# Decay matrices of a gated delta rule on one core: where the per-row factor and its sign are applied

## The reference, cut to what matters

```
S  = S * exp(g_t);  delta = (v_t - k_t.S) * beta_t
S  = S + k_t (x) delta;  o_t = q_t.S          # per head, 8 heads of 128x128
q, k = l2norm(q), l2norm(k);  beta = sigmoid(b);  g = -exp(A_log) * softplus(a + dt_bias)
```

## Time and profile before

| what | value |
|---|---|
| median of 3 runs | 2754.35 us (2753.29 to 2766.41) |
| the profiled execution | 2753.51 us, its span 2751.7 us |
| PE busy | 2447.3 us, 89% of the span |
| DVE busy | 2025.2 us, 74% |
| ACT busy | 1136.2 us, 41% |
| POOL busy | 312.1 us, 11% |
| of POOL, the products of L1251 (64) | 92.3 us, 1475 ns each |
| mean granted TensorE clock | 0.92 of full speed |
| chain that ended last, by engine | PE 57%, DVE 23%, issue 13%, ACT 3%, POOL 1% |

### The profile page before, as it was taken

The page is one execution under the profiler, slowest core; times in us unless marked ns, Lnnn a source line. Parts: engine busy times, 40 slices in busy tenths (PEclk is TensorE's granted clock), DMA queues, the critical chain, the costliest instruction groups (busy, mean ns, idle before and its releaser), DMA issues.

```text
span 2751.7 us, 48745 instructions
## 1 busy us (share of the span) xinstructions
PE 2447.3 (89%) x15408; PEld 1603.4 (58%) x15408; DVE 2025.2 (74%) x6361; ACT 1136.2 (41%) x2066; POOL 312.1 (11%) x236
## 2 busy tenths in 40 slices
PE   2989989898998987898899899899899899899898
PEld 1434444443444444686586586586586586577576
DVE  4858677685867667768768767867867867976976
ACT  0142232313232234446446446446445435545544
POOL 1000000000000002022021121110210211211211
PEclk9989989897988988998998998999999999999899
DMA  5230312213131221201201201201101101211211
GB/s 157 79 94 29 107 41 81 56 62 83 35 109 42 83 55 58 66 14 53 68 9 55 70 2 62 66 6 62 55 17 62 47 25 39 63 32 32 63 39 31
DMA packets 158271, 152.01 MB, mean 55 GB/s; under 512 B 81128, under 2 KB 122672, under 8 KB 157520
## 3 DMA queue, kind: packets, MB, share of 16 engines
q1 hardware_dynamic: 155024, 142.83, 18.0%
q10 hardware_dynamic: 3008, 6.36, 0.6%
HBM read 121.29 MB, written 27.85 MB: 54 GB/s over the span
## 4 chain that ended last, share of the span: by engine, by line
PE 57%; DVE 23%; issue 13%; ACT 3%; DMA 2%; POOL 1%; SPq 1%; DVEq 0%; ACTq 0%; POOLq 0%
PE bank L910 5%; PE bank L922 5%; PE bank L592 4%; PE bank L580 4%; PE bank L583 3%; PE bank L648 3%; DVE arena L1609 3%; PE bank L608 3%; PE bank L502 3%; DVE arena L1667 2%; DVE arena L1665 2%; PE bank L897 2%; DVE arena L1621 2%; PE bank L879 2%; PE bank L870 2%
## 5 line engine op out<-in xcount | busy, mean ns | idle before, releaser
L922 PEld LDWEIGHTS bank<-wring,arena 128*128 128x128 f32 x2048 | 275.6, 199 | 134.6 <-issue 97.3
L1168 ACT ACTIVATE arena<-bank,w_b 128x512 f32<-128x512 f32 x256 | 175.3, 687 | 363.6 <-PE bank L910 363.2
L910 PE MATMUL bank<-arena,wring 128*128 128x512 f32 x512 | 294.1, 661 | 28.7 <-ACT arena L1168 28.6
L922 PE MATMUL bank<-wring,arena 128*128 128x128 f32 x2048 | 281.1, 284 | 22.2 <-DVE arena L1782 15.2
L1609 DVE SCALAR_TENSOR_TENSOR arena<-bank,w_convw,arena 128x511 f32<-128x511 f32 (+2 forms) x384 | 255.0, 741 | 8.7 <-ACT arena L1078 8.5
L1047 ACT ACTIVATE arena<-bank 128x512 f32<-128x512 f32 (+1 forms) x384 | 172.7, 536 | 207.8 <-PE bank L635 206.3
L1453 DVE CUSTOM_DVE_ANT_0 bank<-bank,arena 128x128 f32<-128x128 f32 (+3 forms) x512 | 249.3, 493 | 0.0
L1034 ACT ACTIVATE arena<-bank 128x512 f32<-128x512 f32 x128 | 76.6, 598 | 405.0 <-PE bank L580 405.0
L502 PE MATMUL bank<-w_ident,arena 128*128 128x128 f32 (+2 forms) x652 | 111.6, 298 | 79.5 <-DVE arena L1349 34.1
L592 PE MATMUL bank<-arena 128*128 128x128 f32 x1088 | 163.7, 296 | 0.0
L592 PEld LDWEIGHTS bank<-arena 128*128 128x128 f32 x1088 | 137.7, 198 | 16.6 <-issue 8.9
(11 more groups left out here) (284 smaller groups left out, 4775.5 us busy)
## 6 DMA issues: line engine op xcount, KB each, us to landing
wring<-in_w_last SPq DMA_DIRECT2D x66, 512.0 KB, 3.3
arena<-scrw SPq DMA_DIRECT2D x260, 128.0 KB, 3.0
arena<-scrg SPq DMA_DIRECT2D x32, 512.0 KB, 5.4
arena<-scrq SPq DMA_DIRECT2D x36, 192.0 KB, 3.9
arena<-scrk SPq DMA_DIRECT2D x36, 192.0 KB, 4.5
scrn<-arena SPq DMA_DIRECT2D x64, 64.0 KB, 1.9
arena<-scrn SPq DMA_DIRECT2D x8, 512.0 KB, 3.7
scrx<-arena SPq DMA_DIRECT2D x8, 512.0 KB, 3.4
```

Source lines behind the costliest of these rows:

```text
L910: mm(bank[HBANK[f]][:, :], wring[:, e % 2, k * P:(k + 1) * P], xn1T, start=True, stop=True).then_inc(*s["p_fh"].up)
L922: last = mm(bank[o][:, t * P:(t + 1) * P], GH[:, f % 2, t * P:(t + 1) * P], wring[:, e % 2, FC * P + k * D:FC * P + (k + 1) * D], start=(f ...
L1168: fn(GH[:, f % 2, :], bank[HBANK[f]][:, :], ACT.Gelu_apprx_tanh, bias=W["b1"][:, f:f + 1]).then_inc(*s["a_gh"].up)
```

## The change

The products on POOL go. ACT adds the logarithm of the factor to the exponent instead: exp(G + ln(lam)) = lam * exp(G). Since the bias of an ACT instruction is one number per partition and differs from head to head, each 128x512 exponential becomes four of 128x128. The sign can't be in a logarithm, so `lam` is positive, and the minus signs move: `sub` subtracts, the copies into `Y32` and `Y64` get a scale of -1.0, `so2` adds (and copies where it negated), `lamD` is a plain product.

```diff
 def gam():                                        # ACT
+    act.wait_ge(*s["v_st"].at(b, 1, late))
+    fn(lnlam, lam, ACT.Ln).then_inc(*s["a_lnlam"].up)
     act.wait_ge(*s["v_gT"].at(b, 1, late))
     fn(eG.rearrange("p a b c -> p (a b c)"), bank[0][:, 0:96], ACT.Exp).then_inc(*s["a_eG"].up)
+    act.wait_ge(*s["a_lnlam"].at(b, 1, late))
     for i in range(2 * NT):
         act.wait_ge(*s["v_scan"].at(b, i + 1, late))
-        fn(Gam[:, i, :], Gam[:, i, :], ACT.Exp).then_inc(*s["a_gam"].up)
+        for j in range(4):
+            h = 4 * (i % 2) + j
+            last = fn(Gam[:, i, j * P:(j + 1) * P], Gam[:, i, j * P:(j + 1) * P], ACT.Exp,
+                      bias=lnlam[:, i // 2, h:h + 1])
+        last.then_inc(*s["a_gam"].up)
...
-                fn(Y32[rows], cols(g, 0)[rows], ACT.Copy).then_inc(*s["a_inv"].up)
+                fn(Y32[rows], cols(g, 0)[rows], ACT.Copy, scale=-1.0).then_inc(*s["a_inv"].up)
...
-            fn(Y64[64:P].rearrange("p a b -> p (a b)"), bank[2][64:P, :], ACT.Copy).then_inc(*s["a_inv"].up)
+            fn(Y64[64:P].rearrange("p a b -> p (a b)"), bank[2][64:P, :], ACT.Copy, scale=-1.0).then_inc(*s["a_inv"].up)
...
-def gam():                                        # POOL
-    pool.wait_ge(*s["v_st"].at(b, 1))
-    for i in range(2 * NT):
-        pool.wait_ge(*s["a_gam"].at(b, i + 1))
-        g4 = Gam[:, i, :].rearrange("p (a b) -> p a b", a=4)
-        scale = nlam[:, i // 2, 4 * (i % 2):4 * (i % 2) + 4].unsqueeze(2).broadcast_to((P, 4, P))
-        tt(g4, g4, scale, ALU.mult).then_inc(*s["g_gam"].up)
...
 def stat():                                       # DVE
-    v.scalar_tensor_tensor(out=b4(nlam), in0=rk2b, scalar=-1.0, in1=b4(beta), op0=ALU.mult, op1=ALU.mult
-                           ).then_inc(*s["v_st"].up)
+    link(v.tensor_tensor(b4(lam), rk2b, b4(beta), ALU.mult))
+    v.tensor_scalar(lam, lam, 1e-37, None, ALU.max).then_inc(*s["v_st"].up)
 def stat2():
-    v.scalar_tensor_tensor(out=lamD, in0=nlam, scalar=-1.0, in1=eG[:, 1], op0=ALU.mult, op1=ALU.mult)
+    v.tensor_tensor(lamD, lam, eG[:, 1], ALU.mult)
 def prep(c):
-        dve.wait_ge(*s["g_gam"].at(b, 2 * c + i + 1, late))
+        dve.wait_ge(*s["a_gam"].at(b, 2 * c + i + 1, late))
 def sub(i):
-        last = v.tensor_tensor(Xs[:, 0:n, n:BS], Xs[:, 0:n, n:BS], pr, ALU.add)
+        last = v.tensor_tensor(Xs[:, 0:n, n:BS], Xs[:, 0:n, n:BS], pr, ALU.subtract)
 def so2(c):
-                            bank[4 + i][:, :], ALU.subtract).then_inc(*s["v_o"].up)
+                            bank[4 + i][:, :], ALU.add).then_inc(*s["v_o"].up)
-            v.tensor_scalar(dst, bank[4 + i][:, :], -1.0, None, ALU.mult).then_inc(*s["v_o"].up)
+            v.tensor_copy(dst, bank[4 + i][:, :]).then_inc(*s["v_o"].up)
```

More of the change, by code:

```diff
@@ L277, in build @@
         sse = cut([NT, 8]); rr = cut([NT, 8]); rk2 = cut([NT, HK]); rq2 = cut([NT, HK]); rqs = cut([NT, HK]); rn = cut([NT, HK])
-        nlam = cut([NT, HV]); lamD = cut([NT, HV]); ng0 = cut([NT, HV]); so8 = cut([HV]); rc8 = cut([HV])
+        lam = cut([NT, HV]); lamD = cut([NT, HV]); ng0 = cut([NT, HV]); so8 = cut([HV]); rc8 = cut([HV])
         XT = cut([NT, HV, P]); NTr = cut([NT, HV, P]); QKD = cut([NT, HV, P])
@@ L300, in build @@
         assert max(l0_end, l1_end) <= ARENA, (l0_end, l1_end)
+        lnlam = ng0
         hT, hbuf = qkT[:, 0, :], zz
@@ L310, in build @@
         late_names = """v_var1 g_rstd1 v_xn1 v_ms1 g_rz v_z p_xn1T a_xn1T p_zT v_zT p_ba a_eb v_ab a_eab a_sp v_g p_gc a_eG v_gT
-            p_rf v_lm a_fe v_wf v_glink p_wfT v_wfT p_qkv a_cv v_tap v_cv a_qkv a_sq p_ss v_sse g_rr v_st v_scan a_gam g_gam p_kk v_prep
+            p_rf v_lm a_fe v_wf v_glink p_wfT v_wfT p_qkv a_cv v_tap v_cv a_qkv a_sq p_ss v_sse g_rr v_st v_scan a_gam a_lnlam p_kk v_prep
             v_sub p_z a_sz p_vt a_vb p_inv v_inv a_inv v_tr g_z
@@ L1273, in h1 @@
                     tt(rz, ssq, nhalf[:, 0:NT], ALU.pow).then_inc(*s["g_rz2"].up)
-                steps = {"rr": rr_, "gam": gam, "tr": zeros, "nrm0": nrm0, "nrm1": nrm1, "h1": h1,
+                steps = {"rr": rr_, "tr": zeros, "nrm0": nrm0, "nrm1": nrm1, "h1": h1,
                          "gn": lambda: gn(b, 1), "gx": lambda: gx(b, 1)}
```

## The result

| | before | after |
|---|---|---|
| median of the runs timed side by side | 2757.76 us (2753.29 to 2766.41, 4 runs) | 2800.97 us (2789.76 to 2814.64, 4 runs) |
| span of the profiled execution | 2751.7 us | 2812.5 us |
| PE, DVE busy | 2447.3, 2025.2 us | 2478.3, 2007.5 us |
| ACT, POOL busy | 1136.2, 312.1 us | 1187.2, 220.2 us |

The ratio is 1.0155 (95% interval 1.0128 to 1.0181). The changed kernel is slower, as forecast, but by 43 us, and 2800.97 lies 2 us above the range of 2768 to 2799.

The account below looks back on a forecast made before the run. The prediction took the chain through ACT's last exponential and `gelu 2` to PE's `fo 2` as the bound: 2753.5 us profiled + 24.6 for later exponentials + 8 for PE's clock = 2786 us, range 2768 to 2799.

Parts of the forecast that it names:

- (1) to (5): Profile: scans at 4.6 us, spaced exponentials ending late, PE idle 5 us ahead of `fo 2`, half clock behind.
- (2): On ACT: logarithm of 0.23 us about 0.5 behind L1633, table load, `eG`, 32 exponentials 0.26 to 0.29 us apart.
- (3): On ACT: the last of the 32 exponentials ends 10.5 to 11.5 us after L1633.
- Ahead of the exponentials: On ACT: behind the logarithm and a table load, the first of 32 starts 2.15 us after L1633's start (S).
- The 32 exponentials: On ACT: 0.257 to 0.287 us apart, the last 2.8 to 3.7 us later, taken 3.2; 24.6 us in all.
- The clock: On PE: longer idleness ahead of `fo 2` brings a low clock behind it, nothing to 13.6 us, taken 8.
- (6): Stretch from the first scan to `sub` longer by 3 to 5 us, everything from `sub` on as long as before.
- The power holds DVE: Rival: POOL's power holds up DVE's L1633, everything behind it 5.0 us later an iteration; 2827 us, chance 6%.
- Cheap exponentials: Rival: ACT's exponentials 0.129 us apart end 1.2 us earlier, the gain on DVE comes through; 2744 us, chance 4%.
- Half absorbed: Rival: unseen slack further down on PE or DVE, or better-placed slow clock, leaves 12 us; 2765 us, chance 7%.
- No load of its own: Rival: ACT's logarithm needs no table load, 1.28 us less on the path; 2776 us, chance 1%.
- Signs: Moved minus signs, scaled copies of the merges, `lamD`, `so2` and `sub`: together zero.

Follow-up runs that it names:

- wide8: Changed kernel with 8 exponentials of 128x512 in place of 32, each with the first head's bias for all four heads: 2748.63 us, ratio 0.9964.
- split32: Kernel before, POOL's products kept and no logarithm, each exponential split into four of 128x128 without a bias: 2771.62 us, ratio 1.0030.
- before_b: The kernel before, unchanged, run once more for its profile: 2750.71 us, one run.
- before_c: The kernel before, unchanged, run again for another profile: 2772.46 us, one run.
- r2_before: Kernel before with steps reordered: `fh 2`, `gelu 2` ahead of the exponentials, `prep` and `fo` steps in a new order: 2757.26 us, ratio 0.9985.
- noln: Changed kernel without the logarithm and its wait, `lam` itself taken as the exponentials' bias: 2798.12 us, ratio 1.0141.
- after_c: The changed kernel, unchanged, timed a third time in five rounds: 2801.87 us against 2761.83, ratio 1.0148.
- signs: Kernel before with only the minus signs moved as in the change, products still on POOL: 2764.02 us, ratio 1.0002.

## Why the prediction was right, and why its range was not

**The bound and the mechanism: right in the stage.** ACT was the engine to watch. `fo 2` waits for a gelu that stands behind the exponentials, and wide8 and split32 together show that neither the late start nor the number does it alone. (1) to (5) of the last part came as written, with the distance in (2) and the end in (3) just beyond their upper ends.

**Ahead of the exponentials: right to 0.02.** Logarithm at S + 0.44, load at S + 0.69, first of the 32 at S + 2.13, forecast S + 2.15. The logarithm's load stood in ACT's idle time (1283 ns on average with 0.1 us of idleness for all eight). The 1.38 us of drain that "ScalarE: Activation LUTs" of the Trainium skill gives in "What ACT_TABLE_LOAD costs" didn't appear: the exponential's load ends at 1526.81, and `eG` starts at 1526.82.

**The 32 exponentials: a term that was too small.** I took 0.257 to 0.287 us from start to start, from L1142, and 3.2 us for the shift. It is 0.292 throughout, within groups and between them. The last end is S + 11.58, 0.12 beyond my later bound, and `fo 2` is 3.83 us later in six iterations and 14.77 - 11.46 = 3.31 in the two with slack: 6 x 3.83 + 2 x 3.31 = 29.6 us against the profile that I had, not 24.6. (Between the means of three profiles each it is 28.9, since more iterations of before_b and before_c have slack.) L1142 was the right row for the duration of one (390 ns against 384), but not for the distance, and I had no row for what a bias adds to it: 0.093 us each, by split32. The wide exponential without a bias would have misled more.

**The clock: a term that was too large.** Behind the gap it costs more than I had put in: in the third iteration `fo 2`, `fh 3` and `prep 2` are (2.08 - 1.16) + (1.92 - 1.02) + (2.11 - 1.89) = 2.0 us longer, and summed over eight iterations, between the means of three profiles each, 14.2 us. With the 28.9 of `fo 2` that makes 43.1, and by 43.1 us DVE's taps do start later. But from the taps to `sub` 10.6 us come back. The rows of the taps, before and after (busy us, mean ns | idle before), show where:

```profile
L1609 DVE SCALAR_TENSOR_TENSOR arena<-bank,w_convw,arena 128x511 f32<-128x511 f32 (+2 forms) x384 | 255.0, 741 | 8.7 <-ACT arena L1078 8.5
```

```profile
L1609 DVE SCALAR_TENSOR_TENSOR arena<-bank,w_convw,arena 128x511 f32<-128x511 f32 (+2 forms) x384 | 254.6, 736 | 0.2
```

Before, DVE waited 1.41 to 1.49 us in the middle of the taps, for ACT's copies of `qkv`, in 22 of the 24 iterations of the three profiles (six in this one); after, in none of 24. It waited because PE had a low clock further down in the same stretch, so that the gelus ahead of these copies on ACT came late: in the third iteration the last of them starts at S + 26.38, and in the fourth, where PE keeps the full clock and DVE doesn't wait, at S + 24.95. PE's timeline in the third, before:

```profile
1525.53 1.65 PE L910 MATMUL bank<-arena,wring 128*128 128x512 f32 x2
1526.98 1.92 PE L922 MATMUL bank<-wring,arena 128*128 128x128 f32 x8
1528.68 1.29 PE L910 MATMUL bank<-arena,wring 128*128 128x512 f32 x2
```

In the changed kernel the same work is at or near the full clock:

```profile
1552.61 1.02 PE L911 MATMUL bank<-arena,wring 128*128 128x512 f32 x2
1553.47 1.05 PE L923 MATMUL bank<-wring,arena 128*128 128x128 f32 x8
1554.49 1.13 PE L911 MATMUL bank<-arena,wring 128*128 128x512 f32 x2
```

So the low clock costs 14.2 us in its new place and gives back 10.6 in its old one, a net of 3.6 us where I had put 8. I had named that end ("an existing slow stretch only moves") and had looked only at the two iterations with a slow `prep 1`. The two errors, 4.3 too small and 4.4 too large, cancel: that 24.6 + 8 is the 32.6 us between the means is luck in its parts. Against the one profile that I added to, which has the shortest stage of its three, the stage grew by 340.8 - 305.0 = 35.8.

**The base, and the rest: the step that failed.** I added to one profiled execution of 2753.5 us, and called it as good as the median. In the later comparisons the kernel before has medians of 2757.8, 2758.4, 2762.3 and 2761.8. That is 4 to 9 us more; beside the result it was 2757.8, 4.3 more. Then 7 to 11 us more appear outside the stage, against (6), which said that everything from `sub` on is as long as before. These two make the whole miss: 2801.0 - 2786 = 15 us is 4.3 of base and 43.2 - 32.6 = 10.6 outside the stage, with the stage's own errors cancelled. Either one alone would have left the result inside the range. One place where the longer rest is seen is behind the last iteration: from the last `sub` to the end it is 159.1 us after and 151.6 before, with a stretch there in which PE is never idle and has half its clock (window, us, busy by engine, PEclk, DMA share, GB/s):

```profile
2694.00:2708.00 14.00, 14.00 (x102) 12.84 (x102) 5.37 (x13) 2.54 (x5) 0.00 (x0) 0.52 0.01 1
```

This stretch is not peculiar to the change. r2_before, which has POOL's products, eight exponentials and the old signs, takes 159.2 us from its last `sub` to the end and has such a stretch too:

```profile
2632.00:2646.00 14.00, 13.88 (x119) 11.91 (x116) 6.00 (x14) 3.95 (x9) 0.00 (x0) 0.50 0.10 34
```

And noln, whose total is that of the changed kernel, takes 151.3 there, after_c 154.3. What makes the rest longer is open. For the change: all three rests of after (2459 to 2471 us) are above the mean of before's three, 2448.9, and the timings agree. Against it: before_c has 2459.7, wide8, which has the new signs and the logarithm, 2445.3, and in two kernels without the exponentials' bias, split32 and r2_before, the medians are 10.2 and 9.5 us above what their stages account for, as much as in the changed kernel, while signs and wide8 are only 2 above. So a rest that is some 10 us longer comes with edits that do no work there. It goes loosely with the time that PE has the low clock in the rest, 369 to 460 us in the fourteen profiles (correlation 0.7); what sets that time is not shown. A range should have held such scatter of the profiled execution on both sides; mine ended 13 us above the forecast.

**The rivals.** *The power holds DVE* fell: L1633 starts inside the power's 5.43 us and lasts 0.19, and the scans beside it take 4.56. The Trainium skill, "SBUF — State Buffer", "Summary: rules for kernel authors", would have the second of a GpSimd operation that reads SBUF and a DVE operation with two SBUF inputs fully blocked; the power of the earlier trace rows and this one do not agree with it. *Cheap exponentials* fell by their distance, 0.292 us against the needed 0.168; even without a bias they are 0.199 apart. But its second half is what wide8 showed: with the end at S + 7.13 the gain comes through, 12 us of stage, where I had said 8 x 1.2 = 10. *Half absorbed* was true in kind and too large in size: DVE's wait in the taps was slack that I didn't see, and it took back 10.6 of 43.1 us, but the clock's cost behind the gap had added more than that, and the stage came out at 32.6 and not at 12. *No load of its own* fell by the load at L1095. Signs: zero, as forecast.

## What to carry to other kernels

A product moved off an idle engine into an instruction that is already there is not free: a bias that differs from piece to piece splits the instruction, and the new operand makes all pieces wait for the factor. Price both at the place where the first piece may start, and look at what stands behind the last piece in that engine's order; if something there doesn't depend on them, move it ahead first, since without that a gain elsewhere (here 2.2 us of scans) ends in a wait. And take the base of a sum from several executions, with their scatter in the range on both sides.

## What the runs showed of the hardware

- A bias taken from memory adds 84 to 93 ns to an ACT exponential at either width (625 to 709 ns for 128x512, 297 to 390 for 128x128).
- Such exponentials of 128x128 start 0.292 us apart (0.199 without the bias), and just so where a semaphore that has long been raised stands between two of them: groups of four are 1.17 us apart.
- A table load goes ahead of a single wait (L1095: load with 0.1 us of idleness for eight, then the logarithm with 20.5), but not ahead of the first of two: in noln it idles 3.79 us for `lam`.
- A POOL product of 128x512 slowed DVE's scans from 4.57 to 6.96 us for four, a POOL power of 5.43 us on 128x32 did not slow them at all.
- The clock behind 5.03 to 6.34 us of idleness ahead of `fo 2` fell in all 24 iterations of the three profiles of the changed kernel. With 3.70 us of matmuls put in, `fo 2`, `fh 3` and `prep 2` ran at the full clock in the five iterations with 1.17 to 2.25 us of idleness left, and not in the three with 2.35 to 2.36; in two of the five it fell further down.
